# Graph, state-space and expert layers on one core: cumulated decays as two float32r parts, and another order of GpSimd's list

## What is computed

```python
dt = softplus(dt + dt_bias); A = -exp(A_log)
dA = einsum('bclh,h->bhcl', dtc, A)
A_cum = cumsum(dA, axis=-1)                       # 8 heads x 256 steps
Lmat = exp(where(tril, A_cum[l] - A_cum[s], -inf))
Y_diag = einsum('bcln,bcsn,bhcls,bcshp->bclhp', Cc, Bc, Lmat, xdt)
Y = (Y_diag + xh * D) * silu(z); Y = rmsnorm(Y) * norm_w; out = Y @ W_out @ W_lin + b_lin
```

## Time and profile before

| | |
|---|---|
| time, median of 3 runs | 4072.63 us (4072.6 to 4077.1) |
| the profiled execution's own time | 4071.56 us |
| its span, first to last instruction | 4069.8 us |
| TensorE busy | 3713.7 us, 91% |
| VectorE busy | 2813.6 us, 69% |
| GpSimd busy | 1848.8 us, 45% |
| ScalarE busy | 1794.8 us, 44% |
| first phase (graphs) | to about 3025 us |
| mean granted TensorE clock | 0.949 |

### The profile page before, as it was taken

One profiled execution on the slowest core, in us unless ns is written; L12 is line 12 of the kernel. 1 busy time (PEld: TensorE's weight loads), 2 busy tenths in 40 slices (PEclk: granted clock), 3 DMA queues, 4 the chain that ended last, 5 costly groups with the idle time before them and its releaser, 6 DMA issues.

```text
span 4069.8 us, 67947 instructions
## 1 busy us (share of the span) xinstructions
PE 3713.7 (91%) x20666; PEld 3089.9 (76%) x20666; DVE 2813.6 (69%) x8412; ACT 1794.8 (44%) x3656; POOL 1848.8 (45%) x2019
## 2 busy tenths in 40 slices
PE   5999899989999899998999989989969999999998
PEld 3777777777777777777777777777758888888887
DVE  3877778777787778877788777877844444444444
ACT  2554455544555445554455444545423223333322
POOL 3444444444444444444444444444435545555553
PEclk8999999999999999999999999999979999999999
DMA  2111111111111111010111101001015555555554
GB/s 93 31 31 34 32 43 31 31 34 36 39 31 31 34 36 39 31 34 31 39 36 31 34 31 44 31 31 34 29 47 191 191 198 191 191 197 195 192 192 138
DMA packets 148545, 301.59 MB, mean 74 GB/s; under 512 B 20192, under 2 KB 120800, under 8 KB 130336
## 3 DMA queue, kind: packets, MB, share of 16 engines
q0 software_dynamic: 38272, 196.40, 14.0%
q1 hardware_dynamic: 75424, 71.23, 5.7%
q10 hardware_dynamic: 34816, 33.56, 2.6%
HBM read 248.48 MB, written 52.65 MB: 74 GB/s over the span
## 4 chain that ended last, share of the span: by engine, by line
PE 37%; DVE 28%; POOL 20%; issue 13%; DVEq 1%; DMA 0%; SPq 0%; ACT 0%; POOLq 0%; ACTq 0%
PE bank L1211 12%; PE bank L1225 12%; DVE conv L743 11%; PE bank L1169 9%; POOL masks L428 7%; POOL x1b L459 4%; POOL rstd L421 3%; POOL noedge L435 3%; DVE stats L724 2%; DVE xn L734 2%; PE bank L1161 1%; DVE x L907 1%; POOL x2b L449 1%; DVE z L796 1%; DVE xdt L810 1%
## 5 line engine op out<-in xcount | busy, mean ns | idle before, releaser
L1010 PE MATMUL bank<-xn1T,w_in 128*128 128x256 f32 (+1 forms) x2560 | 605.9, 387 | 46.3 <-DVE conv L743 45.6
L1010 PEld LDWEIGHTS bank<-xn1T,w_in 128*128 128x128 f32 (+1 forms) x2560 | 441.6, 180 | 187.1 <-issue 119.3
L681 ACT ACTIVATE decay<-bank,w_up 128x256 f32<-128x256 f32 x568 | 268.9, 473 | 700.7 <-PE bank L1211 700.7
L449 POOL TENSOR_TENSOR x2b<-x,b_rel 128x256 f32<-128x256 f32 x128 | 90.1, 725 | 979.8 <-DVE xdt L810 971.0
L1211 PE MATMUL bank<-zs,w_up 128*128 128x256 f32 x2272 | 504.5, 380 | 0.6 <-ACT zs L547 0.6
L1225 PE MATMUL bank<-w_dn,decay 128*128 128x256 f32 x2272 | 502.1, 379 | 0.0
L743 DVE SCALAR_TENSOR_TENSOR conv<-bank,conv_w,conv 128x255 f32<-128x255 f32 (+2 forms) x960 | 459.8, 479 | 33.5 <-ACT conv L552 0.7
L1211 PEld LDWEIGHTS bank<-zs,w_up 128*128 128x128 f32 x2272 | 433.3, 191 | 60.3 <-issue 0.9
L1225 PEld LDWEIGHTS bank<-w_dn,decay 128*128 128x128 f32 x2272 | 426.2, 190 | 55.1
L1016 PE MATMUL bank<-w_rel,hT 128*128 128x256 f32 x2048 | 466.4, 381 | 0.7 <-ACT hT L547 0.7
L959 DVE TENSOR_TENSOR hT<-bank,w_dn 128x256 f32<-128x256 f32 x142 | 60.2, 424 | 537.4 <-PE bank L1225 537.4
(11 more groups left out here) (212 smaller groups left out, 7242.0 us busy)
## 6 DMA issues: line engine op xcount, KB each, us to landing
token_rows<-row SPq DMA_DIRECT2D x64, 260.0 KB, 2.6
adj_sb<-in_adj SPq DMA_DIRECT2D x64, 256.0 KB, 3.3
x_sb<-in_x ACTq DMA_DIRECT2D x64, 256.0 KB, 2.7
xT_sb<-in_xT ACTq DMA_DIRECT2D x64, 256.0 KB, 3.0
adjt_sb<-in_adjT SPq DMA_DIRECT2D x64, 256.0 KB, 3.4
out<-row SPq DMA_DIRECT2D x64, 256.0 KB, 2.2
xg<-token_rows,idc POOLq DMA_INDIRECT x142
out<-hT,ids POOLq DMA_INDIRECT x142, 2.4
```

Of the source, the lines that this page charges most:

```text
L681: nc.scalar.activation(hid(f), bank[f % 4][:, 0:GROUP], ACT.Relu, bias=b1[q % 2][:, f:f + 1]).then_inc(hid_ready, 1)
L1010: ins = mm(dst, w_in[:, k, first:first + width], xn1T[:, k, :], start=k == 0, stop=k == DK - 1)
```

## The change

The three bf16 parts `cs3` (72 rows) become two float32r parts `cs2` (40 rows: heads at partitions 0 and 32): VectorE rounds `cs` to float32r, and writes the remainder as float32r. `sel` and `selneg` become float32r; they are built in a float32 view of `decay` and copied by GpSimd before the first round. The six products per head stay, four of them float32r. The gather ring `xg` of the second phase is laid into `w_in`. GpSimd's list is reordered: `x1b` and the edge mask of layer 0 go ahead of the wait for `xdt`, behind a new wait for `part_v` (VectorE's remainder of xn2, L756); the edge mask is made for graph k in round k; the fourth of the relation masks goes behind `rsqrt(3)`. SP loads `adj` of graph k in round k. The last full round is no longer written apart.

```diff
-        sel = sb("sel", [72, H, P], BF16)
-        selneg = sb("selneg", [72, H, N], BF16)
+        sel = sb("sel", [40, H, P], F32R)
+        selneg = sb("selneg", [40, H, N], F32R)
...
-            for i, part in enumerate((0, 32, 64)):
+            for i, part in enumerate((0, 32)):
...
+            pool.wait_ge(built, 3)
+            gp.tensor_copy(sel[:], sel_f)
+            gp.tensor_copy(selneg[:], selneg_f).then_inc(built, 1)
...
-                    ch2.link(dve, v.tensor_copy(cs3[0:H, :], cs[:]), b2_)
-                    ch2.link(dve, v.tensor_tensor(cs_r[:], cs[:], cs3[0:H, :], ALU.subtract), b2_)
-                    v.tensor_copy(cs3[32:32 + H, :], cs_r[:])
-                    ch2.link(dve, v.tensor_copy(cs_m[:], cs_r[:]), b2_)
-                    v.tensor_tensor(cs3[64:64 + H, :], cs_r[:], cs_m[:], ALU.subtract).then_inc(cs_ready, 1)
+                    ch2.link(dve, v.tensor_copy(cs2[0:H, :], cs[:]), b2_)
+                    v.tensor_tensor(cs2[32:32 + H, :], cs[:], cs_hi, ALU.subtract).then_inc(cs_ready, 1)
...
-                        mm(o[:, first:first + width], sel[:, h, :], cs3[:, l:N], start=True, stop=False)
+                        mm(o[:, first:first + width], sel[:, h, :], cs2[:, l:N], start=True, stop=False)
                         mm(o[:, first:first + P], identb[:], negmask[:], start=False, stop=False,
                            skip_group_check=True)
-                        ins = mm(o[:, first:first + width], cs3[:, s:s + P], selneg[:, h, 0:width], start=False,
+                        ins = mm(o[:, first:first + width], cs2[:, s:s + P], selneg[:, h, 0:width], start=False,
                                  stop=True)
```

More of the change, by code:

```diff
@@ L163, in graph_mamba_moe @@
         dt_pos, dt, dA, cs = sb("dt_pos", [H, N]), sb("dt", [H, N]), sb("dA", [H, N]), sb("cs", [H, N])
-        cs3 = sb("cs3", [72, N], BF16)
-        cs_r, cs_m = sb("cs_r", [H, N]), sb("cs_m", [H, N], BF16)
+        cs2 = sb("cs2", [40, N], F32R)
+        cs_hi = cs2[0:H, :].bitcast(F32)
         xdt = pair("xdt", F32, DIN)
@@ L211, in graph_mamba_moe @@
         ids, idc = sb("ids", [P, TG, P], I32), sb("idc", [P, TG, P], I32)
-        xg = [sb(f"xg_{i}", [P, TG, ROW]) for i in range(RING)]
+        ring = w_in[:, :, :].rearrange("p k n -> p (k n)")
+        xg = [ring[:, i * TG * ROW:(i + 1) * TG * ROW].rearrange("p (j d) -> p j d", d=ROW) for i in range(RING)]
         xgn = xdt[:, 0, :].rearrange("p (j d) -> p j d", d=D)
@@ L319, in graph_mamba_moe @@
         pool_engine = [None]
-        def is_last(b):
-            return isinstance(b, int) and b == NB - 1
         def rounds(eng, step):
@@ L328, in rounds @@
             step(1, 0, None)
-            with eng.Fori(2, NB - 1) as k:
+            with eng.Fori(2, NB) as k:
                 step(k, k - 1, k - 2)
-            step(NB - 1, NB - 2, NB - 3)
             step(None, NB - 1, NB - 2)
@@ L353, in step @@
             def step(b1_, b2_, b3_):
-                if b1_ is not None and not is_last(b1_):
-                    sp.wait_ge(noedge_ready, b1_ + 1)
-                    sp.dma_start(adj[:], adj_v[b1_ + 1]).then_inc(adj_in, 16)
+                if b1_ is not None:
+                    need(sp, noedge_ready, b1_)
+                    sp.dma_start(adj[:], adj_v[b1_]).then_inc(adj_in, 16)
                 if b2_ is not None:
@@ L364, in step @@
                     sp.dma_start(rows_v[b3_], row[:]).then_inc(rows_out, 16)
-            sp.dma_start(adj[:], adj_v[0]).then_inc(adj_in, 16)
             step(0, None, None)
             step(1, 0, None)
-            with sp.Fori(2, NB - 1) as k:
+            with sp.Fori(2, NB) as k:
                 step(k, k - 1, k - 2)
-            step(NB - 1, NB - 2, NB - 3)
             step(None, NB - 1, NB - 2)
@@ L383, in _ @@
             gp.memset(row[:], 0.0)
-            gp.memset(cs3[:], 0.0)
+            gp.memset(cs2[:].bitcast(F32), 0.0)
             for a, v in ((cpos, 1e4), (cneg, -1e4), (czero, 0.0)):
@@ L387, in _ @@
             gp.memset(negmask[:], 0.0)
-            gp.memset(sel[:], 0.0)
-            gp.memset(selneg[:], 0.0)
+            gp.memset(sel_f, 0.0)
+            gp.memset(selneg_f, 0.0)
             gp.memset(identb[:], 0.0)
@@ L421, in rsqrt, with edge_masks @@
                 gp.tensor_tensor(rstd[i][:], ve[i][:], mhalf[:], ALU.pow).then_inc(rstd_ready[i], 1)
[L423 to L437, removed]
+            def edge_masks(first, last):
+                for r in range(first, last):
+                    ins = gp.tensor_scalar(masks[:, :, r, :], adjt[:], float(r + 1), None, ALU.is_equal)
+                return ins
             def step(b1_, b2_, b3_):
@@ L441, in step @@
                     rsqrt(0, b1_)
+                if b3_ is not None:
+                    pool.wait_ge(part_v, b3_ + 1)
+                if b2_ is not None:
+                    if isinstance(b2_, int) and b2_ == 0:
+                        pool.wait_ge(loads, 16 * len(small))
+                        pool.dma_start(w_up[0][:], io["moe_up"][0:P, :]).then_inc(up_in[0], 16)
+                        pool.dma_start(w_dn[0][:], io["moe_dn"][0:P, :]).then_inc(dn_in[0], 16)
+                    pool.wait_ge(x1_ready, b2_ + 1)
+                    need(pool, x2_ready, b2_)
+                    for t in range(T):
+                        last = gp.tensor_tensor(x1b[:, t, :], x1[:, t, :], b_lin[:], ALU.add)
+                    last.then_inc(x1b_ready, 1)
+                if b1_ is not None:
+                    pool.wait_ge(adj_in, 16 * (b1_ + 1))
+                    need(pool, e_ready, b1_)
+                    carry(pool)
+                    gp.tensor_scalar(noedge[:], adj[:], 0.0, NEG_BIG, ALU.is_le, ALU.mult).then_inc(noedge_ready, 1)
                 if b2_ is not None:
@@ L451, in step @@
                 if b2_ is not None:
[L452 to L461, removed]
+                    pool.wait_ge(adjt_in, 16 * (b2_ + 1))
+                    carry(pool)
+                    edge_masks(0, R - 1)
                 if b3_ is not None:
                     rsqrt(3, b3_)
-                if b1_ is not None and not is_last(b1_):
-                    pool.wait_ge(e_ready, b1_ + 1)
-                    no_edge(b1_ + 1)
+                if b2_ is not None:
+                    edge_masks(R - 1, R).then_inc(masks_ready, 1)
                 if b1_ is not None:
```

8 lines of the change are left out of this document (5 added, 3 removed).

## The result

The kernel after takes 4412.87 us (4411.99 to 4413.22, 4 runs) against 4072.61 us of the kernel before: a ratio of 1.083 (95% interval 1.0815 to 1.0852). It is 340 us slower. The forecast was 3934 us, 138 faster. All that is slower together had been given a chance of 0.10. The measured time lies near the rival in which float32r pays plain float32's price (4388 us), but, as the experiments show, not for that reason.

The account below looks back on a forecast made before the run. The prediction took a GpSimd pole, then a clock loss, with TensorE's dense part right behind, to bound each 45.9 us round. 62 x (2.64 - 0.4) = 139, less 1, under 4071.6 gave 3934 us, range 3865 to 4066.

Parts of the forecast that it names:

- the rival in which float32r pays plain float32's price: Expo's float32r products cost as plain float32 at any width: 1.52 us a head, 4388 us; chance 0.06.
- What bounds the kernel: First-phase rounds of 45.9 us: a GpSimd pole, behind it a clock loss, TensorE's dense part right behind these two.
- GpSimd's list: x1b and noedge, 2.85 + 2.09 us, move into GpSimd's idleness; the 2.6 us between ve(1) and rstd(1) are gone.
- My own rival without TensorE's cost: Float32r weights load as fast as bf16's, so hp stays put: 62 x 3.2 = 198 us, 3874; chance 0.13.
- the two prices given: x1b, moved ahead of xdt on GpSimd, costs 1.41 us (x2b's price) to 2.85.
- The reason given for the fourth mask: With rstd(3) 0.7 and the fourth mask 1.6 behind it, GpSimd is free before ve(1) to start rstd(1).
- VectorE's split: VectorE's L788 to L792 shrink from 1.79 to about 0.75 us, ahead of z, e and xdt; TensorE gets nothing.
- The products of expo: TensorE's expo heads take 0.61 us instead of 0.45, float32 weights loaded under the product before: +1.26 us a round.
- The upper end of my bounds: Expo's products as plain float32: 0.43 us at 256 columns and 0.22 at 128, 1.52 a head.
- The clock: TensorE's low spell keeps half its length in half of the rounds, costing about 0.8 on L1169: 0.4 us a round.
- The sum: 62 x (2.64 - 0.4) = 139, less 1 for the ends: 138 us faster, 3934 us.
- What would show it wrong: Heads 0.45 or 0.88 and more apart, L1169 still 5 us and more, e waiting for noedge, or masks still in the chain.

Follow-up runs that it names:

- e1: Kernel after with the three bf16 parts and bf16 selections of 72 rows put back, GpSimd's new list kept: 3834.2 us, ratio 0.942.
- e9: e1 with the fourth relation mask put back beside the other three, ahead of rstd(3): 3861.0 us, ratio 0.949.
- e7: Kernel after with cs2, sel and selneg on 72 rows instead of 40, the added rows zero: 3941.6 us, ratio 0.968.
- e12: Kernel before with float32r parts on 72 rows and GpSimd's old list: 3971.0 us, ratio 0.975.
- e3: Kernel after with cs2, sel and selneg on 128 rows instead of 40, the added rows zero: 3944.4 us, ratio 0.969.
- e10: Kernel after, float32r on 40 rows, with the mask products also cut to 40 rows and the decays scaled by 0.001: 3985.2 us, ratio 0.979.
- e6: e1 with two bf16 parts on 40 rows, the mask products cut to 40 rows too and the decays scaled by 0.001: 3861.4 us, ratio 0.948.

## Why the prediction was wrong

*What bounds the kernel, and GpSimd's list*: right. e1 shows the gain alone, 3.65 us a round. My own rival without TensorE's cost had 3.2 (198 us, 3874), against 3834 measured. In the kernel after rstd(1) waits for ve(1), and x1b took 1.44 us, the lower of the two prices given. The reason given for the fourth mask was wrong: it matters through weigh (e9), not through rstd(3).

*VectorE's split*: 0.75 forecast, 0.73 measured, hidden as said in the new list: e7 is over e1 by all that TensorE's heads cost, 8 x 0.21 = 1.7 us a round. In the old one it isn't (e12).

*The products of expo*: here it failed. The step went from columns and weight loads to "0.61 a head". For float32r beside products of its own row count that was nearly right: 0.66 (e3, e7, e10). What it put at nothing, without a word, is that 40 rows instead of 72 stand beside the 128 rows of the mask products, four changes in a head. Each makes the next weights load late, so that "loaded under the product before", on which the sum rests, doesn't hold there. In the place of 0.16 us a head the runs show 0.21 for the type (e7 less e1) and 0.45 for the changes (after less e7): over eight heads 1.7 and 3.6 us a round. The upper end of my bounds, plain float32 at 1.52, was never touched; that 4388 came near is chance.

*The clock*: the step "one spell of half today's length in half of the rounds" fell too. The spell in the tail is gone, better than hoped, but a group of stalling heads brings the low clock on itself: L1012 and L1131 each 1.4 us longer. Without the stalls the step was near: in e7 a record of L1165 takes 431 ns over 500 to 2900 us, against 545 in the kernel before and 392 in the kernel after.

```profile
L1165 PE MATMUL bank<-w_proj,y 128*128 128x256 f32 x864 | 240.9, 431 | 16.6 <-DVE y L852 13.6
```

I had asked only where idleness ends, not where the change makes the work thin.

*The sum*: without the changes of row count it holds. e7 is the change as I had pictured it, and takes 3941.6 us where 3934 was forecast, a round of 43.91 against 43.7. Part of this is luck: the list gives 3.65 us a round (e1) where the sum had 3.2, and the type costs 1.66 (e7 less e1) where the sum had 1.0, which is 198 less 138 us over 62 rounds. The two misses go opposite ways. From e7 to the kernel after it is 7.3 us a round: 3.6 in the heads, 2.8 by the clock behind them, 0.7 at the ends of the groups (e10 less e7), and 0.2 not accounted for.

*What would show it wrong*: "heads 0.45 or 0.88 and more apart" did. The rule of TensorE: Matmul & The Clock Gate of the Trainium skill (Weight-path perf modes) on the fast weight load, read by the letter, would have kept float32r at 0.45: e7 has 0.66, and its float32r loads take 192 ns against 98 of bf16, so float32r doesn't get it here. That float32r weights load as plain float32's, as I took it from L1183, stands.

The best version of all is e1, the bf16 parts under the new list: 3834.2 us, 5.8% under the kernel before and 13% under the kernel after.

## What to carry to other kernels

Before the number of an operand's partitions is changed, look at the products beside it on TensorE: if they then differ in rows, every change between 40 and 128 rows costs about 0.1 us here, which is twice a narrow bf16 product, and padding with rows of zeros, to 72 or to 128 (e7, e3), cost nothing. A shorter split on VectorE is worth nothing if the engine that gets the operands is the next pole. And when a gap on TensorE closes, count the clock that comes back with it; when short products begin to stall, count the clock that goes.

## What the runs showed of the hardware that I had not expected

- A change between products of 40 and of 128 rows stalls TensorE by 0.10 us, in bf16 (0.45, 0.65 and 0.86 us a head with no, two and four changes) and by 0.11 in float32r (0.66 to 1.11). The next weights then load with their product and not under the one before. 72 beside 128 rows doesn't stall. TensorEngine Tiling of the Trainium skill (When to Use Tiling) counts a contraction of up to 64 rows as row tiling. That 40 and 72 fall on two sides of such a line agrees with the trace. The same page (Key Properties) says that changing the tiling mode drains TensorE, and has no figure for it; the 0.10 us agrees with such a drain, but no run shows that the mode is what changes here. Where between 40 and 72 the step lies wasn't tried.
- Float32r products of 256 and 128 columns stand in the trace as one record each, with 0.18 to 0.20 and 0.06 to 0.14 us to the next start, not the 0.43 and 0.22 of plain float32. Their weights load as slowly as plain float32's, 192 ns against 98 of bf16.
- The lower clock stood behind each group of stalling heads, though TensorE counts as busy throughout (3.40 of 3.40 us in the stretch shown): here a busy share of TensorE in the profile said nothing of its clock. Why stalling products bring the lower clock stays open; few active rows don't (e6, e10).
- With nothing but the operands' rows and the clock behind it, one and the same arithmetic took from 3942 to 4413 us (e7 and after).
